# Criss-cross attention on 512 channels of 96 x 96: residual loads issued in the column stage, the last tile of a unit finished behind half of the next unit's low parts, and four steps placed elsewhere

## What is computed

```python
q = einsum('oc,bchw->bohw', Wq, x) + bq
k = einsum('oc,bchw->bohw', Wk, x) + bk
v = einsum('oc,bchw->bohw', Wv, x) + bv
energy_H = einsum('bchw,bcgw->bhwg', q, k) - 1e30 * eye(H)
energy_W = einsum('bchw,bchv->bhwv', q, k)
att = softmax(concatenate([energy_H, energy_W], -1), -1)
att_H, att_W = att[..., :H], att[..., H:]
out_H = einsum('bcgw,bhwg->bchw', v, att_H)
out_W = einsum('bchv,bhwv->bchw', v, att_W)
return gamma * (out_H + out_W) + x
```

## Time and profile before

| | us |
|---|---|
| median of 3 runs (3816.43 to 3822.62) | 3816.54 |
| the profiled execution's own time | 3821.81 |
| its span | 3820.1 |
| PE busy in it | 3699.6 (97%) |
| DVE, ACT, POOL busy | 2743.3, 1545.3, 692.1 |
| granted TensorE clock, mean | 0.989 |

### The profile page before, as it was taken

How to read it: one execution, slowest core, us unless ns; L and a number is a source line. 1 busy time by engine, 2 the same in 40 slices (tenths; PEclk the granted TensorE clock), 3 DMA queues, 4 the chain that set the end, 5 groups by cost and what they waited for, 6 DMA issues and landing times.

```text
span 3820.1 us, 63188 instructions
## 1 busy us (share of the span) xinstructions
PE 3699.6 (97%) x24664; PEld 3383.3 (89%) x24664; DVE 2743.3 (72%) x4900; ACT 1545.3 (40%) x2322; POOL 692.1 (18%) x816
## 2 busy tenths in 40 slices
PE   8799999999999999999999999999999999999999
PEld 7798989889898898988989889898898989989888
DVE  8767787577875778757786577865778667786555
ACT  8523454235542445424454144541444414444111
POOL 1410033100321003210032100420004200042000
PEclk9999999999999999999999999999999999999999
DMA  7777758777587775877759777597776977659665
GB/s 265 189 219 255 259 187 232 220 245 262 193 230 224 242 256 192 237 218 258 266 168 250 220 264 260 170 261 220 256 241 185 250 229 259 236 186 252 209 211 177
DMA packets 337398, 873.70 MB, mean 229 GB/s; under 512 B 35024, under 2 KB 191184, under 8 KB 337104
## 3 DMA queue, kind: packets, MB, share of 16 engines
q1 hardware_dynamic: 337104, 869.67, 73.5%
HBM read 661.92 MB, written 207.62 MB: 228 GB/s over the span
## 4 chain that ended last, share of the span: by engine, by line
PE 91%; DVE 5%; DMA 1%; ACT 1%; issue 1%; DVEq 0%; POOL 0%; SPq 0%; ACTq 0%; POOLq 0%
PE bank L1099 42%; PE bank L1066 18%; PE bank L1087 15%; PE bank L1015 10%; PE bank L1027 3%; PE bank L1036 3%; DVE Sy L775 2%; DMA XT_r<-in_x_row 1%; DVE E L792 1%; DVE Y L866 1%; DVE Y L857 1%; DVE mx_c L787 0%; PE bank L1012 0%; ACT Sy L665 0%; DVE zs_c L802 0%
## 5 line engine op out<-in xcount | busy, mean ns | idle before, releaser
L1099 PE MATMUL bank<-Sy,Wv_hi 128*128 128x512 f32 x4608 | 1463.7, 399 | 22.4 <-DVE Sy L775 22.4
L1099 PEld LDWEIGHTS bank<-Sy,Wv_hi 128*128 128x128 f32 x4608 | 851.6, 190 | 182.7 <-issue 23.7
L1099 PE MATMUL bank<-Sy,Wv_lo 128*128 128x512 f32 x2304 | 908.2, 394 | 0.0
L866 DVE SCALAR_TENSOR_TENSOR Y<-bank,bv_sb,Y 128x384 f32<-128x384 f32 (+2 forms) x1152 | 502.6, 478 | 539.0 <-PE bank L1099 539.0
L1087 PE MATMUL bank<-Pt,XT_r 128*128 128x96 f32 x6144 | 732.6, 276 | 28.0 <-DMA XT_r<-in_x_row 16.5
L1087 PEld LDWEIGHTS bank<-Pt,XT_r 128*128 128x128 f32 x6144 | 719.2, 193 | 37.8 <-DMA XT_r<-in_x_row 17.9
L533 POOL TENSOR_TENSOR Pe<-Pe,F 128x384 f32<-128x384 f32 x336 | 301.8, 905 | 2332.1 <-DMA Pe<-e_scratch 2278.2
L665 ACT ACTIVATE Sy<-Y 128x256 fp32r<-128x256 f32 (+2 forms) x576 | 320.2, 618 | 756.9 <-PE bank L1099 708.1
L1099 PEld LDWEIGHTS bank<-Sy,Wv_lo 128*128 128x128 f32 x2304 | 436.2, 189 | 96.7
L652 ACT ACTIVATE Y<-bank 128x384 f32<-128x384 f32 x384 | 326.4, 850 | 456.2 <-PE bank L1066 456.2
L639 ACT ACTIVATE E<-E 96x384 f32<-96x384 f32 x384 | 201.1, 524 | 756.0 <-DVE E L792 755.3
(11 more groups left out here) (73 smaller groups left out, 2907.9 us busy)
## 6 DMA issues: line engine op xcount, KB each, us to landing
XT_r<-in_x_row SPq DMA_DIRECT2D x384, 384.0 KB, 4.6
Y<-in_x SPq DMA_DIRECT2D x192, 768.0 KB, 6.7
XA<-in_x SPq DMA_DIRECT2D x180, 768.0 KB, 5.1
out<-Y SPq DMA_DIRECT2D x176, 768.0 KB, 3.7
XT_r<-in_x_col SPq DMA_DIRECT2D x192, 384.0 KB, 8.1
XT_c<-in_x_col SPq DMA_DIRECT2D x192, 384.0 KB, 7.9
e_scratch<-E SPq DMA_DIRECT2D x384, 144.0 KB, 2.7
Pe<-e_scratch SPq DMA_DIRECT2D x336, 144.0 KB, 5.6
```

The source lines that it names most:

```text
L866: last = nc.vector.scalar_tensor_tensor(to, proj_ps[c % 2][:, at:at + width], bv_sb[:, c:c + 1], to, op0=ALU.add, op1=ALU.add)
L1099: last = nc.tensor.matmul(proj_ps[c % 2][:, :], w[:, ct, at], Sy[:, lo, ct, :], start=(ct == 0 and k == 0), stop=(ct == CT - 1 and k == 2))
```

## The change

It has five parts. (1) `load_xres(b, 0)` and `load_xres(b, 1)` are issued in the column stage, right behind the third load of row pieces, and no longer between the loads 4, 5 and the next weights of the row stage. (2) In DVE's order the first low half of unit u + 1 stands before the finish of tile 3 of unit u; where rows follow, the second stands behind the first added row as before; for unit 17, where none follow, it stands right behind the finish, and the shift and sum of slot 3 come behind it. (3) POOL's scaling of the weights for unit u + 3 waits until the first tile of unit u is summed. (4) ACT's first two query gathers stand one slot earlier, before the exponential of the last chunk of row energies. (5) The second key and query chunk of unit 5 stands at slot 2 instead of 3.

```diff
-A_SLOTS = {5: (1, 3, 4), **{u: (0, 2, 4) for u in range(6, A_LAST + 1)}}
+A_SLOTS = {5: (1, 2, 4), **{u: (0, 2, 4) for u in range(6, A_LAST + 1)}}
@@ SP, column_stage
                             load_xtr(b, i - PIECES)
+                    if 2 * g + CRING + 2 == PIECES + RRING + 1:
+                        load_xres(b, 0)
+                        load_xres(b, 1)
@@ SP, row_stage
                 load_xtr(b, RRING)
                 load_xtr(b, RRING + 1)
-                load_xres(b, 0)
                 load_xtr(b, RRING + 2)
-                load_xres(b, 1)
                 load_p(b, CHUNKS + PRING + 1)
@@ POOL, row_stage
                     kq, split, group = stage_plan(more)
+                    if turned_for(u + 3):
+                        pool.wait_ge(proj_summed, past(proj_summed, (b * UNITS + u) * CT + 1))
                     for n in turned_for(u + 3):
                         scale(b, CHUNKS + n)
@@ ACT, row_stage, after(slot)
                             round_x(b + 1, x_next, 1)
+                        if group(u, slot + 1) == 0:
+                            gather_q(b + 1, 0)
+                            gather_q(b + 1, 1)
                         if m is not None:
                             exponentials(b + 1, m)
-                        if g == 0:
-                            gather_q(b + 1, 0)
-                            gather_q(b + 1, 1)
@@ DVE, row_stage
+                    rows = rows_of(u + 2)
                     for c in range(CT):
                         low_x_after(c)
+                        if c == CT - 1 and u + 1 < UNITS:
+                            low_y(b, u + 1, 0)
                         finish(b, u, c)
+                        if c == CT - 1 and u + 1 < UNITS and not rows:
+                            low_y(b, u + 1, 1)
                         shift_after(c)
...
-                    rows = rows_of(u + 2)
-                    for h in range(HALVES):
-                        if u + 1 < UNITS:
-                            low_y(b, u + 1, h)
-                        for i in rows[h:h + 1]:
-                            add_row(b, i)
+                    if rows:
+                        add_row(b, rows[0])
+                        low_y(b, u + 1, 1)
+                        add_row(b, rows[1])
                     low_x_after(AFTER_TILES)
-                    for i in rows[2:3]:
-                        add_row(b, i)
+                    if rows:
+                        add_row(b, rows[2])
                     shift_after(AFTER_TILES)
```

## The result

| | before | after |
|---|---|---|
| median, us (lowest to highest of 4) | 3817.77 (3816.43 to 3822.62) | 3782.62 (3777.94 to 3795.35) |
| profiled execution, its own time and span | 3821.81, 3820.1 | 3782.12, 3780.4 |
| PE busy | 3699.6 | 3687.7 |

A forecast was written before the change was run, and what follows sets the result against it. TensorE was taken as the bound, busy 3699.6 of 3820.1 us, leaving 120 us of stands and slow clock behind them. Terms summed to -50.5: 3771.3 for the profiled execution, 3766 for the median, range 3748 to 3794.

The forecast's parts named there:

- -9: First rows of the row stage: moving the residual loads cuts PE's stands from 22.3 to 13 us, 9 us saved.
- -3: First rows of the row stage: one stand in place of two leaves some of the clock, 3 us saved.
- rival B: Row stage: the residual pair delays load 3, PE stands longer at row 6, +7 us, 3785 in all; chance 0.17.
- -3.5: Behind the query gathers: slow clock after PE's stand goes in about half the batches, 3.5 us saved.
- -10: Two terms, 10 us saved each: first low half before the finish (unit 17), and slot 2 for slot 3 in unit 5.
- +2: Units of column energies: ACT's half comes 0.1 to 0.3 us late for the low half, 2 us lost, bounds 0 and +10.
- D: Rival: DVE stands for ACT's rounding before a finish at 136 places; at 0.5 us each the time is 3834; chance 0.04.
- -4.5: Behind unit 4: POOL's scalings, made to wait, no longer slow the low half and added rows, 4.5 us saved.
- -12.5: End of unit 12: query gathers ahead of ACT's exponential end PE's wait for them in seven batches, 12.5 us saved.

The follow-up runs named there:

- e4: The kernel before with only the two residual loads moved into the column stage: ratio 1.0036 to the kernel before, median 3833.1 us.
- e2: The changed kernel with both residual loads behind all three row pieces of the row stage: ratio 0.9809 to the kernel before, median 3748.3 us.
- e3: The changed kernel with DVE's former order (finish, shift, sum, both low halves) in units 13 to 15: ratio 0.9873 to the kernel before, median 3773.2 us.
- e5: The kernel before with only POOL's scaling made to wait for the unit's first tile: ratio 0.9976 to the kernel before, median 3809.2 us.
- e6: The changed kernel with residual loads behind all three row pieces and without POOL's scaling wait: ratio 0.9831 to the kernel before, median 3752.8 us.

## Why the prediction was right or wrong

**Residual loads: wrong, and in sign.** The step that failed is "about 1 us of stand in three batches like batch 0 and 2 us in the other five: 13 us in place of 22.3, -9", with "-3" for the clock. Measured: 29.4 in place of 22.3, +7, and in e4 +14 us of time. The mechanism was rival B's, to which I gave 0.17; its time, 3785, is nearer to the 3783 measured than the 3766 of the forecast, and that the forecast's own band reaches to 3785 does not make its mechanism right. That B's +7 is exact is in part luck: it was summed from five stands of 4.9 us and three of 1.6, and the stands were 1.5 to 4.7 in one profile and 0.9 to 5.0 in the other.

The mis-sized term is the surplus of the pair over the room. I took 4.5 us for the pair, near the fast end of 4.0 to 6.7. Load 3 alone took 3.1 to 3.4 us to land before. In batch 1, with 1.8 us of room, it landed after 7.3 and 8.6 us in the two profiles, 4 and 5.3 later than alone. By this estimate the pair held the queue for 5.8 to 7.1 us there, at the slow end of my span or past it. The room was overrated as well, in batch 0: I counted all missing tenths between the full slices as free, and one empty slice too many. The earlier trace rows has four zeros, not five, which makes 68 tenths or 4.4 us. The last two digits, 1 and 6, lie behind the issue of load 3 at 226.5, so they are its own start and no room for what is ahead of it; without them 55 tenths, 3.6 us, are left. That is less than my own 4.5 for the pair. The Trainium skill (DMA: Bandwidth & Descriptors, section on queues, rings and completion order) says that each DMA engine consumes its descriptors in ring order. The traces agree: load 3 landed after 3.1 to 3.7 us without the pair in front (before and e2), and after 4.4 to 8.6 behind it.

**The clock: about right in sum, by terms that were not.** Forecast "-3.5" and "-3"; the busy time fell by 11.9 and 5.7 us in the two profiles. The "-3" had the wrong sign: the first rows lacked 12 us of the full clock before and 20 after, by the estimate given with e2. I also sized the excess there at 1 us a batch, 8 in all, where e2, which has none, shows 12 to be had. The "-3.5" was too small: behind the gathers the clock was granted at 0.66 for 5 us in three of seven batches before, 1.7 us each, and at 1.00 in the place of the earlier trace rows after. The rest of the gain was not traced to places.

**Low halves: right in mechanism, under-sized.** "-10" and measured 22.4 to 5.7 plus a new entry of 1.3 for a finish, 15.4 less. I had the first half start PE at 594.2, 0.5 us behind the energies, and the second at 596.4, 0.8 behind the first half's end; PE stood only 0.30 and 0.28, since a low half takes 1.29 us there and not the 1.45 that I had, and PE follows it sooner.

**Its price in the units of column energies: right place, wrong size.** "+2 ... bounds 0 and +10". It is 10.8 us of waits in three units a batch, and the 5.3 of before, which lay behind unit 4, are gone besides, so all of the 10.8 is new and over the upper bound; e3 takes it back. I had looked at the 0.1 to 0.3 us by which ACT is late, and not at what a later second half runs beside on POOL, though rows 8 showed that price in another place. Of the rivals D is nearest, with 21 places instead of 136.

**Scaling: right in mechanism, half in size** by itself (-4.5; e5 -9, of which 5.3 are waits). Beside the new order e6 shows 2.5 us of waits for it; its time there is open.

**Query gathers and slot: right.** -12.5 and -10, measured 12.4 and 11.4 of waits. The low parts of x did not come late.

**Sum.** Row pieces +7, low halves and finish -15, evictions -11, gathers -12, added rows +5.5, idle elsewhere -1, busy time -12: -39 of the span's 39.7. The forecast of -50.5 is for this same execution, so 11 us are missing in the profile and 16 to 17 in the medians. The row pieces alone missed by 16, and the added rows by 8 (+5.5 for -4.5 and +2); the low halves and the clock gave about 5 each more than forecast and evictions 1 more. That the missing time looks like the row pieces alone is these others cancelling.

## What to carry to other kernels

A transfer moved ahead of others on one queue was paid for here by the first one behind it that was needed soon: ask what that one's landing time is alone, and count as room in the queue only time in which nothing is on its way. Look at every batch for it, and at more than one execution. In this kernel the large loads that are needed late belong behind the small ones that are needed at once, even though these can be issued only later. When an operation changes place in one engine's order, look at what runs beside its new place on an engine that competes with it, not only at who waits for it.

## What was not expected

A stand of PE cost more than its own length: with 26.6 us of it gone, 10 to 17 us of busy time went too, and the window behind one stand of 4.51 us showed a granted clock of 0.50 for 6 us. The stands of one batch differed by up to 3.3 us between two profiles of the same kernel, and their sum by 0.5. And the median of the kernel before differed by 0.15% between the three chips (3817.6 to 3823.2), which is more than half of what the smallest part is worth; only ratios to a kernel run on the same chip could tell the parts.
